# A transformer-like chain on one core: the experts' second linear with its weights stationary

## What is computed

```python
x = h.reshape(T, D)                      # T = 4096, D = 128, layer norm of x
idx = jnp.argmax(softmax(x @ gate_w + gate_b)); prb = its probability
buf = zeros((E, C, D)).at[idx, pos].set(x, mode='drop')        # E = 8, C = 640
hmid = relu(einsum('ecd,edf->ecf', buf, w1) + b1[:, None, :])   # F = 512
ybuf = einsum('ecf,efd->ecd', hmid, w2) + b2[:, None, :]
y = nan_to_num(ybuf[idx, pos] * (prb * kept)[:, None], nan=0.0, posinf=10000.0, neginf=-10000.0)
```

## Time and profile before

| | |
|---|---|
| median of 3 runs | 1069.16 us (1068.97 to 1069.34) |
| the profiled execution | 1073.89 us, its span 1072.2 us, mean granted clock 0.990 |
| TensorE busy in the span | 1020.4 us (95%) |
| VectorE, ScalarE, GpSimd busy | 563.1, 320.8, 225.9 us |
| second linear of the experts, L1727 | 320 records, 37.9 us busy |
| first linear of the experts, L1717 | 128 records from 618.0 us on |
| from the first B to the last B | 623.2 to 694.7 us |

### The profile page before, as it was taken

One profiled execution on the slowest core, in us unless ns is written; L12 is line 12 of the kernel. 1 busy time (PEld: TensorE's weight loads), 2 busy tenths in 40 slices (PEclk: granted clock), 3 DMA queues, 4 the chain that ended last, 5 costly groups with the idle time before them and its releaser, 6 DMA issues.

```text
span 1072.2 us, 12873 instructions
## 1 busy us (share of the span) xinstructions
PE 1020.4 (95%) x3642; PEld 536.4 (50%) x3642; DVE 563.1 (53%) x1539; ACT 320.8 (30%) x627; POOL 225.9 (21%) x217
## 2 busy tenths in 40 slices
PE   4989999999999999999999899959999999999997
PEld 1435555555455544444444377723454554454544
DVE  6688888888821234434334444553543534435365
ACT  3654764664521100000000053404223123132231
POOL 4011331332322012122121224443110110100101
PEclk9999999999999999999999999979999999999999
DMA  9969855655200488888872663236664655555400
GB/s 360 408 237 316 285 203 227 235 225 209 117 1 1 157 303 310 321 297 314 302 300 100 261 216 92 82 85 235 236 227 176 236 187 213 195 204 193 157 1 20
DMA packets 45357, 220.98 MB, mean 206 GB/s; under 512 B 6626, under 2 KB 27940, under 8 KB 33634
## 3 DMA queue, kind: packets, MB, share of 16 engines
q1 hardware_dynamic: 42146, 215.60, 54.2%
q0 software_dynamic: 2864, 4.39, 1.2%
q10 hardware_dynamic: 272, 0.13, 0.0%
HBM read 210.68 MB, written 11.62 MB: 207 GB/s over the span
## 4 chain that ended last, share of the span: by engine, by line
PE 78%; DVE 12%; DVEq 3%; issue 3%; DMA 2%; ACT 2%; POOL 1%; SPq 0%; another core or an unknown queue 0%; POOLq 0%; ACTq 0%
PE PA L1545 31%; PE PA L1750 20%; DVE R L928 7%; PE O L1727 3%; PE O L1793 3%; PE O L1588 3%; PE PA L1508 2%; DMA ring<-in_adj_cols 2%; PE T L1802 1%; PE SR L1793 1%; PE T L1813 1%; PE SM L1793 1%; PE PA L1717 1%; PE O L1772 1%; ACT U L667 1%
## 5 line engine op out<-in xcount | busy, mean ns | idle before, releaser
L1750 PE MATMUL PA<-ring,S 128*128 128x512 f32 x512 | 233.4, 596 | 2.2 <-ACT S L682 2.2
L1545 PE MATMUL PA<-ring,S 128*128 128x512 f32 x512 | 229.8, 597 | 0.1
L1545 PE MATMUL PA<-ring,U 128*128 128x512 f32 x512 | 226.2, 595 | 0.0
L1545 PEld LDWEIGHTS PA<-ring,U 128*128 128x128 f32 x512 | 94.9, 190 | 107.2 <-issue 107.1
L1545 PEld LDWEIGHTS PA<-ring,S 128*128 128x128 f32 x512 | 96.0, 191 | 103.5 <-issue 101.5
L928 DVE TENSOR_TENSOR R<-R,ring 128x1024 f32<-128x1024 f32 x98 | 138.9, 1418 | 7.1 <-issue 1.8
L1750 PEld LDWEIGHTS PA<-ring,S 128*128 128x128 f32 x512 | 92.1, 190 | 100.6 <-issue 96.1
L576 ACT ACTIVATE work<-ring 128x2048 int8<-128x2048 f32 x64 | 122.3, 1910 | 42.0 <-DMA ring<-in_adj_cols 38.6
L1414 DVE TENSOR_TENSOR U<-ring,work 128x512 f32<-128x512 f32 x112 | 84.2, 759 | 85.1 <-PE SR L1793 42.1
L868 POOL DMA_DIRECT2D out_x<-work x7 | 5.9, 844 | 233.1 <-DVE work L1485 233.1
L827 POOL DMA_INDIRECT disp_d<-work x32 | 32.0, 999 | 96.5 <-DVE work L1260 89.1
(11 more groups left out here) (241 smaller groups left out, 1157.4 us busy)
## 6 DMA issues: line engine op xcount, KB each, us to landing
ring<-in_adj_cols SPq DMA_DIRECT2D x56, 2048.0 KB, 7.6
ring<-in_adjT_cols SPq DMA_DIRECT2D x32, 2048.0 KB, 7.3
work<-in_w SPq DMA_DIRECT2D x16, 256.0 KB
ring<-in_Wr SPq DMA_DIRECT2D x1, 4096.0 KB, 13.6
ring<-in_Wr SPq DMA_DIRECT2D x2, 2048.0 KB, 18.1
disp_d<-U SPq DMA_DIRECT2D x4, 650.0 KB, 10.3
work<-disp_d SPq DMA_DIRECT2D x8, 325.0 KB
S<-in_x SPq DMA_DIRECT2D x4, 512.0 KB, 5.9
```

Source lines behind the costliest of these rows:

```text
L1545: mm = nc.tensor.matmul(out_T[:, :], X[:, t * D:(t + 1) * D], ring[slot][t // HT][:, (t % HT) * BW:(t % HT + 1) * BW], start=n == 0, stop= ...
L1750: mm = nc.tensor.matmul(PA[slot][:, :], S[:, t * D:(t + 1) * D], ring[1][t // HT][:, (t % HT) * BW:(t % HT + 1) * BW], start=t == 0, stop= ...
```

## The change

The second linear turns its operands round: `w2` of a feature group f is stationary (128 x 128) and the activations move, 384 and 256 columns at a time, so that 4 products fill each bank and y lies with its features on the partitions. The first linear's halves become the same 384 and 256 columns. ScalarE adds `b2` as a bias per feature while it reads a bank into `e_yT` (`add_b2`, `s_yT`), one expert late in its list: behind the copies of the next expert's rows, ahead of its ReLUs. TensorE turns `e_yT` back into rows, into the same banks O (`turn_y`, `s_yt`), after the fourth product of the next expert's A, and after the last B for the last expert. VectorE then scales straight out of the banks; its bias add is gone. The first half of B waits for seven ReLUs, the second for the eighth. `b2` comes as one column, and the weights of expert e wait for ScalarE's adds of the expert before the last. `e_yT` takes 640 columns of U that lay free in this stage.

```diff
@@ -169,13 +169,14 @@
         e_w1 = [part(early, F1), part(at, F1)]
         e_w2 = [part(early + F1, FK * D), part(at + F1, FK * D)]
         at = 7 * BW
-        e_b2 = [part(early + F1 + FK * D, D), part(at, D)]
+        e_b2 = [part(early + F1 + FK * D, 1), part(at, 1)]
         e_b1 = [part(early + F1 + FK * D + D, FK), part(at + D, FK)]
         at += D + FK
         e_idx = [part(at + 8 * i, CT).bitcast(U32) for i in range(2)]
         at += 16
         e_xT = U[:, 0:CAP]
         e_hm = U[:, CAP:(1 + FK) * CAP]
+        e_yT = U[:, (1 + FK) * CAP:(2 + FK) * CAP]
         e_y = [R[:, CAP * i:CAP * (i + 1)] for i in range(2)]
         e_lim, e_sub = [R[:, CAP * (2 + i):CAP * (3 + i)] for i in range(2)]
         e_odd = R[:, CAP * 4:CAP * 5].bitcast(I32)
...
@@ -508,7 +511,7 @@
                 sp.dma_start(e_w1[par], A["w1"][ds(e, 1)].rearrange("o p f -> (o p) f")).then_inc(s_ein[par], 16)
                 sp.dma_start(e_w2[par], A["w2"][ds(e, 1)].rearrange("o p f -> (o p) f")).then_inc(s_ein[par], 16)
                 sp.dma_start(e_b1[par], A["b1"][ds(e, 1)].rearrange("o p f -> (o p) f")).then_inc(s_ein[par], 16)
-                sp.dma_start(e_b2[par], A["b2_bc"][ds(e, 1)].rearrange("o p f -> (o p) f")).then_inc(s_ein[par], 16)
+                sp.dma_start(e_b2[par], A["b2_cols"][ds(e, 1)].rearrange("o p f -> (o p) f")).then_inc(s_ein[par], 16)
 
             sp.wait_ge(s_clean2, NB)
             alone(sp)
...
@@ -533,7 +536,7 @@
                 sp.wait_ge(s_tags, e - 1)
                 alone(sp)
                 load_rows(e, e % 2)
-                sp.wait_ge(s_ye, e)
+                sp.wait_ge(s_yT, 2 * (e - 1))
                 alone(sp)
                 load_weights(e, e % 2)
 
...
@@ -660,15 +663,24 @@
                 act.wait_ge(s_xTp, e + 1)
                 nc.scalar.copy(e_xT[:, 0:BW], T[0][:, :])
                 nc.scalar.copy(e_xT[:, BW:CAP], T[1][:, 0:CAP - BW]).then_inc(s_xT, 1)
+                if e > 0:
+                    add_b2(e - 1, 1 - par)
                 act.wait_ge(s_ein[par], (e // 2 + 1) * 64)
                 for q in range(2 * FK):
-                    f, c = q // 2, q % 2
+                    f, (lo, hi) = q // 2, EPARTS[q % 2]
                     act.wait_ge(s_h1, e * (2 * FK) + q + 1)
-                    nc.scalar.activation(e_hm[:, f * CAP + c * CAP // 2:f * CAP + (c + 1) * CAP // 2], HB[q % 4][:, 0:CAP // 2],
+                    nc.scalar.activation(e_hm[:, f * CAP + lo * P:f * CAP + hi * P], HB[q % 4][:, 0:(hi - lo) * P],
                                          ACT.Relu, bias=e_b1[par][:, f:f + 1]).then_inc(s_hm, 1)
+
+            def add_b2(e, par):
+                for n, (lo, hi) in enumerate(EPARTS):
+                    act.wait_ge(s_yp, e * 2 + n + 1)
+                    alone(act)
+                    nc.scalar.activation(e_yT[:, lo * P:hi * P], O[n][:, 0:(hi - lo) * P], ACT.Identity, bias=e_b2[par][:, 0:1]).then_inc(s_yT, 1)
 
             for e in range(E1):
                 expert(e, e % 2)
+            add_b2(E1 - 1, (E1 - 1) % 2)
 
 
             act.wait_ge(s_wts3, 16 * len(F2_INPUTS))
...
@@ -1302,50 +1314,43 @@
 
             def expert(e, par, rnd):
 
-                def read(n):
+                def scale(n):
 
                     lo, hi = EPARTS[n]
-                    dve.wait_ge(s_yp, e * 2 + n + 1)
+                    dve.wait_ge(s_yt, e * 2 + n + 1)
                     alone(dve)
-                    return nc.vector.tensor_tensor(tiles(e_y[par][:, lo * D:hi * D], hi - lo), tiles(O[n][:, 0:(hi - lo) * D], hi - lo),
-                                                   e_b2[par].unsqueeze(1).to_broadcast([P, hi - lo, D]), ALU.add)
-
-                def scale(n):
-                    for q in range(*EPARTS[n]):
-                        yq = e_y[par][:, q * D:(q + 1) * D]
-                        nc.vector.tensor_scalar(yq, yq, e_tags[par][:, q, 0:1], None, ALU.mult)
-                    dve.drain()
-
-                def finite(n, between=None):
+                    for q in range(lo, hi):
+                        last = nc.vector.tensor_scalar(e_y[par][:, q * D:(q + 1) * D], O[n][:, (q - lo) * D:(q - lo + 1) * D],
+                                                       e_tags[par][:, q, 0:1], None, ALU.mult)
+                    return last
+
+                def finite(n):
 
                     lo, hi = EPARTS[n]
                     y, odd, lim, sub = [v[:, lo * D:hi * D] for v in (e_y[par], e_odd, e_lim, e_sub)]
                     nc.vector.tensor_scalar(odd, y, 0.0, 0.0, ALU.mult, ALU.not_equal)
                     nc.vector.tensor_scalar(lim, y, BIG, -BIG, ALU.min, ALU.max)
                     dve.drain()
-                    if between is not None:
-                        between()
                     nc.vector.scalar_tensor_tensor(sub, y, INF, lim, ALU.is_le, ALU.mult)
                     dve.drain()
                     nc.vector.copy_predicated(y, odd, sub).then_inc(s_y, 1)
                     dve.drain()
 
-                dve.wait_ge(s_yp, e * 2 + 1)
-                alone(dve)
                 if rnd is not None:
                     dve.wait_ge(s_sc2[par], rnd * (16 * CT))
                     alone(dve)
 
                 nc.vector.tensor_copy(e_idx[par], e_tags[par][:, :, 1])
-                read(0)
-                dve.drain()
                 scale(0)
                 if e < E1 - 1:
-                    read(1).then_inc(s_ye, 1)
+                    scale(1).then_inc(s_ye, 1)
+                    dve.drain()
                     finite(0)
                 else:
-                    finite(0, lambda: read(1))
-                scale(1)
+                    dve.drain()
+                    finite(0)
+                    scale(1)
+                    dve.drain()
                 finite(1)
 
             for e in range(2):
...
@@ -1712,26 +1717,34 @@
                 pe.wait_ge(s_ein[par], rnd * 64 + 64)
                 pe.wait_ge(s_xT, e + 1)
                 for q in range(2 * FK):
-                    f, c = q // 2, q % 2
+                    f, (lo, hi) = q // 2, EPARTS[q % 2]
                     pe.wait_ge(s_hm, e * (2 * FK) + q + 1)
-                    nc.tensor.matmul(HB[q % 4][:, 0:CAP // 2], e_w1[par][:, f * P:(f + 1) * P], e_xT[:, c * CAP // 2:(c + 1) * CAP // 2],
+                    nc.tensor.matmul(HB[q % 4][:, 0:(hi - lo) * P], e_w1[par][:, f * P:(f + 1) * P], e_xT[:, lo * P:hi * P],
                                      start=True, stop=True).then_inc(s_h1, 1)
+                    if q == 3 and e > 0:
+                        turn_y(e - 1)
                 if more:
                     turn_rows(1 - par, rnd + par)
-                pe.wait_ge(s_hm, e * (2 * FK) + 2 * FK + 4)
                 pe.wait_ge(s_ye, e + 1)
-                for bank, (lo, hi) in zip(O, EPARTS):
+                for n, (lo, hi) in enumerate(EPARTS):
+                    pe.wait_ge(s_hm, e * (2 * FK) + 2 * FK + 3 + n)
+                    for f in range(FK):
+                        mm = nc.tensor.matmul(O[n][:, 0:(hi - lo) * P], e_w2[par][:, f * D:(f + 1) * D], e_hm[:, f * CAP + lo * P:f * CAP + hi * P],
+                                              start=f == 0, stop=f == FK - 1)
+                    mm.then_inc(s_yp, 1)
+
+            def turn_y(e):
+                for n, (lo, hi) in enumerate(EPARTS):
+                    pe.wait_ge(s_yT, e * 2 + n + 1)
                     for q in range(lo, hi):
-                        c = q - lo
-                        for f in range(FK):
-                            mm = nc.tensor.matmul(bank[:, c * D:(c + 1) * D], e_hm[:, f * CAP + q * P:f * CAP + (q + 1) * P],
-                                                  e_w2[par][:, f * D:(f + 1) * D], start=f == 0, stop=f == FK - 1)
-                    mm.then_inc(s_yp, 1)
+                        last = nc.tensor.transpose(O[n][:, (q - lo) * D:(q - lo + 1) * D], e_yT[:, q * P:(q + 1) * P], ident[:, :])
+                    last.then_inc(s_yt, 1)
 
             keep_warm(12, S[:, 0:BW], PA[0])
             turn_rows(0, 0)
             for e in range(E1):
                 expert(e, e % 2, e // 2, e < E1 - 1)
+            turn_y(E1 - 1)
 
 
             pe.wait_ge(s_sc2[1], 16 * CT * E1 // 2)
```

More of the change, by code:

```diff
@@ L333, in build @@
         s_yp = sem("s_yp")
+        s_yT = sem("s_yT")
+        s_yt = sem("s_yt")
         s_ye = sem("s_ye")
@@ L1890 @@
         "b1": g["L0_ffn_b1"].reshape(E1, FK, P).transpose(0, 2, 1),
-        "b2_bc": _np.broadcast_to(g["L0_ffn_b2"][:, None, :], (E1, P, D)),
+        "b2_cols": g["L0_ffn_b2"][:, :, None],
         "gnn_W": g["L1_gnn_W"].reshape(P, 1),
```

## The result

Timed side by side on one chip, the kernel before takes 1069.16 us and the kernel after 1072.53 (medians of 10 runs each): a ratio of 1.0041, 95% interval 1.0028 to 1.0054. The change makes the kernel slower by 0.4%, 3.4 us, where 1.4 were forecast.

A forecast was written before the change was run, and what follows sets the result against it. TensorE's instructions were taken to bound the expert stage: first B 0.2 earlier, seven periods +1.0, end +0.6, together +1.4 on 1069.16, giving 1070.6 us. The forecast's own range was 1069.0 to 1072.9, with rivals 1065.3 to 1073.0.

The forecast's parts named there:

- The sum for the expert stage: Experts, undisturbed: first B 0.2 earlier, seven periods of 9.80 instead of 9.66 (+1.0), end +0.6; together +1.4 us.
- B: An expert's second linear on TensorE: 16 records instead of 40 take 4.32 us instead of 4.57, 0.25 less.
- The wait for ReLU 7: Ahead of the second linear: its first half no longer waits for the last ReLU, 0.2 us gained an expert.
- Turning back: Five transposes of y an expert on TensorE, after the next first linear's fourth product: 0.55 us added, their waits hidden.
- First B: Expert 0's second linear starts 0.2 us earlier, by the wait on ReLUs gained.
- The end: From the last second linear's start to its first scatter: 8.64 us instead of 8.00, a cost of 0.6.
- The bubbles: Possible small losses at new waits in each expert's period: 9.80 us taken, 9.70 with none, 10.05 with 0.1 at three.
- From the first scatter on nothing changes: Everything behind the last expert's first scatter, the last stage included, was taken to keep its time.
- The cause of the hold: TensorE's signals come late while GpSimd's scatters run, 5.0 us together; blamed on the profile's recording, so absent from timed runs.
- Rival 1: Expert stage: the hold is real in timed runs and 16 records end it; 3.6 us gained, 1065.6; chance 0.28.
- Rival 2: Expert stage: the hold is real and stays, moved with the later scatters; 6 to 15 us slower, about 1076; chance 0.07.
- What was named as evidence: Trace after: 9.8 us periods, last B near 691.6, first scatter 700.2, span near 1068.6, profile and median within 1 us.

The follow-up runs named there:

- e1: Kernel after with 39 more VectorE instructions that only count a semaphore up, ahead of the last stage: 1071.29 us, 1.0023 of the kernel before.
- e13: Kernel before without the scatters of experts 0 to 6 and the waits on them, on a fourth chip: 1069.19 us, 0.9959 of the kernel before.
- e6: Kernel before, unchanged, recorded again on a second chip: 1069.22 us.
- e4: Kernel before with only the first linear in parts of 384 and 256 columns and separate waits for ReLU 7 and 8: 1067.31 us, 0.9986.
- e16: Kernel before with only the second linear's operands changed round (16 records), no turning back, on a fifth chip: 1067.97 us, 0.9945 of the kernel before.
- e17: Kernel after with 39 more VectorE instructions and its second linear as 20 products of 128 columns (40 records): 1075.38 us, 1.0009 of the kernel before.
- e7: Kernel after with 39 more VectorE instructions and the turning back of y left out: 1064.58 us, 0.9949 of the kernel before.
- e2: Kernel before with 89 more VectorE instructions ahead of the last stage: 1073.55 us, 1.0047 of the kernel before.
- e5: Kernel before with 50 more VectorE instructions ahead of expert 0 and 39 ahead of the last stage: 1071.98 us, 1.0020.
- e9: Kernel after, unchanged, on a third chip: 1073.27 us, 0.9990 of the kernel before.
- e10: Kernel after with 39 more VectorE instructions, on the third chip: 1071.85 us, 0.9973 of the kernel before.
- e11: Kernel after with 30 more VectorE instructions, on the third chip: 1071.01 us, 0.9966 of the kernel before.
- e12: Kernel before, unchanged, recorded on a fourth chip: 1074.87 us.
- e15: Kernel after with 39 more VectorE instructions, on the fourth chip: 1071.15 us, 0.9975 of the kernel before.
- e14: Kernel before with the split first linear and separate waits for ReLU 7 and 8, on the fourth chip: 1074.00 us, 0.9990 of the kernel before.
- e18: Kernel after with 35 more VectorE instructions and the last expert in the old form, on a sixth chip: 1070.90 us, 0.9951 of the kernel before.

## Why the prediction failed, step by step

**The sum for the expert stage comes out near, by terms that don't, and that is luck.** It said +1.4 from the first A to the first scatter. In e1 it is 87.31 from A's first record to the last scatter, against 85.90 to 85.95 in undisturbed executions of the kernel before (e13, e6): +1.4, of which 1.2 stand at the first scatter. Its terms:

- B: -0.16 instead of -0.25. I divided 4.57 by 40 and had 114 ns a record; but in those 4.57 lies what B loses at its start to the ReLU. Without it B takes 4.49 (e4), 112 ns a record. The 4.32 that I worked out for the new form measured 4.33; e16 (9.66 to 9.50) and the first period of e17 (9.73 to 9.90) give the same 0.16 and 0.17. The Trainium skill, "TensorE: Matmul & The Clock Gate" ("Wait — 56ns, not 53.3ns?"), gives each product at 2.4 GHz a fixed 2.5 ns or so beside its columns, measured on bf16. An estimate by that figure, taken for each record, is 0.06 for 24 records less; the trace has 0.16, so there is a surcharge by count here too, and a larger one.
- The wait for ReLU 7, with the shorter last ReLU: -0.31 (e4) instead of -0.2. Together with B this gives -0.47 where I had -0.45.
- Turning back: +0.55, as forecast (e7). Waits at its sides: none. So the period is 9.66 - 0.16 - 0.31 + 0.55 = 9.74, measured 9.73; I had 9.76 and took 9.80.
- First B 0.23 earlier (4.93 after A instead of 5.16), forecast 0.2.
- The end: 8.95 instead of 8.64, against 8.01. From the last B to VectorE's first scale it is 5.02 where I had 4.86, since the turning starts 4.38 after B and VectorE 0.64 later; and from there to the scatter 3.93 where I had 3.78, since L1332 takes 0.56 here and 0.35 in expert 0.
- The five last scatters: 5.38 from the first to the last instead of 5.16; not in the sum.

Seven times 0.07, less 0.23, plus 0.94 and 0.22, is 1.42. The bubbles that I put in and that weren't there paid for the tail that I had too short.

**"From the first scatter on nothing changes": this step failed**, and with it the forecast of no measurable difference: the sum had nothing for what a shorter VectorE list does to the last stage. Six blocks of 42.28 instead of 41.94 are 2.04, the part behind the last block's start 71.55 instead of 71.13 another 0.42: 2.46. Against e6 the whole is +1.4 to the last scatter, +0.5 to block 0, -0.7 in block 0, +2.5 behind it: 3.6 from the first A to the end, and the timed runs have 3.4. e1, e2, e5, e9, e10 and e11 show that the position in VectorE's list does it. Not all of it comes back with 39 more instructions: on one chip the timed gain is 1.4 (e9, e10) where the trace has 2.4, with 30 more it is 2.3 (e11); that the instructions cost time themselves would explain it, and isn't shown. The later blocks are also what the trace lost between its last scatter and its end. The measured 1072.53 lies inside the range that the forecast gave itself (1069.0 to 1072.9), but by chance: that range was for bubbles in the seven periods and for a longer end of the stage, with nothing in it for what stands behind.

**The cause of the hold failed as well.** I took it for a thing of the recording, because the profiled time stood 4.73 above the median. The two were from executions with and without the hold, and the difference is real time. The kernel before takes 1069.2 to 1069.5 on two chips, and its trace there has no hold (e6, with more instructions e2, e5); it takes 1074.3 to 1076.8 on four others, and where it was recorded on one its trace has it (e12). The Trainium skill's "NOTIFIC — the notification-queue block", section 7.1 (Overflow: three behaviours, one of which stalls the engine), on which I leaned, says that the block holds its producers back inside rather than lose a record. It doesn't decide this: by my reading of it the timed runs would have no hold, and e12 and e13 time it at 0.4% (0.2 to 0.6). What else the writing of records does isn't settled either: each timed execution comes with a span and a granted clock of its own, so that no run shows one of which nothing was recorded.

**Rival 1 was right in its mechanism on those chips, and wrong on the one that was timed.** It said that 16 records are sparse enough and that the change gains 3.6. On chips with the hold e15 is 0.25% below the kernel before and e11 0.34%, 2.7 to 3.6 us; the kernel after as it is loses most of it again to the stop (0.9990). To judge by its 1069.16, the timed comparison ran on a chip without the hold, with nothing to gain. **Rival 2** didn't come with 16 records: 10.24 (e9) is the longest period that the new form showed. With 40 (e17) the hold does come back beside the moved scatters, with periods up to 10.73.

**What was named as evidence.** Last B 690.62 (691.6 forecast), first scatter 699.57 (700.2), both within 1.0; the span 1070.2 instead of 1068.6, which is the stop. Profile and median within 1 us of each other, as I had written, and yet for another reason: an agreement that a wrong cause predicts as well doesn't test it. Recording the kernel before a second time would have.

## What to carry to other kernels

When a profiled execution is longer than the median, look whether one of its stretches has two periods, and take both as real until a second recording says otherwise. An edit that takes instructions from an engine's list moves everything behind it: compare a stage that the edit doesn't touch as well, and where it changed by the same amount in each turn of a loop, try some empty instructions ahead of it. And a short product costs by its columns plus a little by its count, so that fewer, longer products gain less than the count says; what they save is easily spent on turning the result back (0.16 against 0.55 here).

## What the runs showed of the chip

- In the blocks of the last stage VectorE's sequencer stands still for about 0.35 us once in 128 instructions, at fixed numbers of its list (2368, 2496 and so on). Where TensorE waits on VectorE right there, a block of 41.93 takes 42.28; 39 or 30 empty instructions switch that off, 89 in the kernel before switch it on (e1, e11, e2). What the engine does in this time isn't shown, nor whether the rest of the list has such stops.
- Beside GpSimd's indirect scatters, TensorE's signals behind a run of 40 records of 112 ns come over a microsecond late (e12: the second read 1.9 after the next A has started, where it is 0.3 in e6). With 16 records of 0.27 on average (4.33 / 16) nothing of it is seen at the old place (e16), and 0.3 to 0.9 us of the whole stage in the new form (e15, e9). By the times of the kernel before this is so on four of six chips, and on one of them its trace shows it (e12). Why these and not the others stays open, and whether it goes with the chip or with what else ran there: each was visited once.
- Under that hold the period was set by a circle through GpSimd (3.13 + 5.11 + 2.18), so that 0.31 an expert taken from TensorE gained nothing (e14). In the last expert, a single run of 40 records behind seven sparse experts, it didn't occur (e18).
